# The small matmuls of a step gathered at its end, and the attention and expert work moved into the other halves of two PSUM banks

## The reference, cut to what matters

```python
# mixer, per sequence (chunks of 32 tokens in the reference; the kernel takes a sequence of 64 as one)
proj = input_states @ in_proj_w.T                 # gate, xBC, dt
xBC = silu(conv(moveaxis(xBC, 1, 2), 4 taps) + conv_b)
scores = einsum('bcihn,bcjhn->bcijh', Cc, Bc) * Ldec * dtc
y = einsum('bcijh,bcjhp->bcihp', scores, xc) + state part + D * x
g = y * silu(gate);  g = gg * rsqrt(mean(gg*gg) + eps) * norm_w    # 8 groups of 1024
x = x + g @ out_w.T
# attention: 8 kv heads, 4 repetitions, 16 dims, keys = values = ctx
scores = einsum('bsgrd,btgd->bgrst', xq, xk) / sqrt(16) + mask
x = x + einsum('bgrst,btgd->bsgrd', softmax(scores), xv)
# experts: 4 of rank 16, the best 2 of them weighted
x = x + sum_e gates[e] * (mid[e] @ B[e].T) * 4
```

## Time and profile before

| | |
|---|---|
| three runs | 3002.11, 3005.6, 3007.3 us |
| the profiled execution | 3009.73 us, span 3007.9 us |
| PE busy | 2905.6 us, 97% |
| DVE busy | 2024.6 us, 67% |
| ACT, POOL busy | 1366.0 us (45%), 1251.1 us (42%) |
| chain that ended last | PE 92%, DVE 5% |
| mean granted TensorE clock | 0.979 |

### The profile page before, as it was taken

One profiled execution on the slowest core, in us unless ns is written; L12 is line 12 of the kernel. 1 busy time (PEld: TensorE's weight loads), 2 busy tenths in 40 slices (PEclk: granted clock), 3 DMA queues, 4 the chain that ended last, 5 costly groups with the idle time before them and its releaser, 6 DMA issues.

```text
span 3007.9 us, 56310 instructions
## 1 busy us (share of the span) xinstructions
PE 2905.6 (97%) x22224; PEld 2292.7 (76%) x22224; DVE 2024.6 (67%) x3144; ACT 1366.0 (45%) x2025; POOL 1251.1 (42%) x820
## 2 busy tenths in 40 slices
PE   3999999999999999999999999999999999999986
PEld 2777777777778777787877778787777877777764
DVE  4787777787666657776666665777566665666656
ACT  2556556555443443443444444344344344444422
POOL 2666666666333433333333333433333343333332
PEclk7999999999999999999999999999999999999985
DMA  5787787778655655655665565655565565565510
GB/s 180 258 269 266 256 270 254 244 261 268 194 173 184 189 179 168 189 184 174 203 188 174 188 189 161 190 181 176 185 197 185 172 191 182 168 194 183 172 36 15
DMA packets 179267, 578.27 MB, mean 192 GB/s; under 512 B 25216, under 2 KB 31872, under 8 KB 170816
## 3 DMA queue, kind: packets, MB, share of 16 engines
q1 hardware_dynamic: 179008, 574.66, 59.8%
HBM read 460.29 MB, written 114.29 MB: 191 GB/s over the span
## 4 chain that ended last, share of the span: by engine, by line
PE 92%; DVE 5%; ACT 1%; issue 1%; DMA 1%; POOL 0%; SPq 0%; ACTq 0%; DVEq 0%; POOLq 0%
PE p_in L431 53%; PE p_out L431 23%; PE p_y L431 10%; PE p_in L510 4%; DVE cv L1125 1%; PE p_y L601 1%; DVE o_ring L1067 1%; ACT w_ring L763 0%; DVE acb L1184 0%; DVE sm L1271 0%; DVE cpar L1108 0%; ACT o_ring L763 0%; DVE sc L1259 0%; DMA decay<-cum_scr 0%; PE p_y L620 0%
## 5 line engine op out<-in xcount | busy, mean ns | idle before, releaser
L431 PE MATMUL p_in<-xnb,w_ring 128*128 128x512 f32 x6912 | 1735.3, 401 | 13.8 <-DVE cv L1125 9.6
L431 PEld LDWEIGHTS p_in<-xnb,w_ring 128*128 128x128 f32 x6912 | 1263.5, 189 | 286.3 <-issue 14.7
L1447 POOL TENSOR_TENSOR g_lo<-g_f,g_hi 128x512 fp32r<-128x512 f32 x256 | 375.6, 1467 | 1248.5 <-ACT g_hi L763 1248.5
L1125 DVE SCALAR_TENSOR_TENSOR cv<-p_in,cpar,cv 128x504 f32<-128x504 f32 (+2 forms) x960 | 703.4, 733 | 118.7 <-ACT cv L763 94.9
L431 PE MATMUL p_out<-o_ring,g_hi 128*128 128x512 f32 x2048 | 648.1, 397 | 0.0
L763 ACT ACTIVATE cv<-p_in,cpar 128x512 f32<-128x512 f32 x320 | 247.9, 777 | 734.3 <-PE p_in L431 689.7
L1160 DVE SCALAR_TENSOR_TENSOR t_y<-x_t,dpar,p_y 128x256 f32<-128x256 f32 x512 | 222.8, 476 | 397.6 <-PE p_y L431 395.2
L431 PEld LDWEIGHTS p_out<-o_ring,g_hi 128*128 128x128 f32 x2048 | 382.4, 188 | 91.1
L763 ACT ACTIVATE sg<-p_in 128x512 f32<-128x512 f32 x256 | 153.5, 600 | 628.3 <-PE p_in L431 628.2
L431 PE MATMUL p_out<-o_ring,g_lo 128*128 128x512 f32 x1024 | 405.4, 396 | 0.0
L1149 DVE TENSOR_TENSOR x_tok<-p_in,dts 128x512 f32<-128x512 f32 x256 | 176.9, 691 | 299.0 <-PE p_in L510 295.5
(11 more groups left out here) (233 smaller groups left out, 2244.3 us busy)
## 6 DMA issues: line engine op xcount, KB each, us to landing
w_ring<-ws_scr SPq DMA_DIRECT2D x432, 512.0 KB, 3.4
o_ring<-ows_scr SPq DMA_DIRECT2D x192, 512.0 KB, 3.4
ws_scr<-w_ring SPq DMA_DIRECT2D x144, 512.0 KB, 4.8
decay<-cum_scr SPq DMA_DIRECT2D x128, 512.0 KB, 6.6
raw_w<-wt SPq DMA_DIRECT2D x144, 256.0 KB, 4.1
ows_scr<-o_ring SPq DMA_DIRECT2D x64, 512.0 KB, 6.2
raw_o<-owt SPq DMA_DIRECT2D x64, 256.5 KB, 5.4
acb<-x SPq DMA_DIRECT2D x3, 1024.0 KB, 7.8
```

The costliest lines, as they stand in the source:

```text
L431: return nc.tensor.matmul(o, lhsT=l, rhs=r, start=first, stop=last)
L1125: ins = V.scalar_tensor_tensor(acc[:, :, t:SEQ], src[:, :, 0:SEQ - t], cpar[:, 5 * m + 3 - t:5 * m + 4 - t], acc[:, :, t:SEQ], ALU.mult, A ...
L1447: T(g_lo[:, c % 2, :], g_f[:, c % 2, :], g_hi[:, c % 2, :].bitcast(F32), ALU.subtract).then_inc(glo_done, 1)
```

## The change

The work is the same; places, buffers and order change.

- `p_in`, `p_y` and `p_out` become single tensors, and every slot now writes to `free`, columns 256 to 511 of the two `p_y` banks, beside the columns that `heads` uses. A slot of PE no longer waits for `yread`. Instead ACT's slot waits for it (`heads_read`) before it reads the banks, and DVE's `skipped` waits until the step's slot is written (`slot_written`).
- PE's step is A, B, `project`, `heads`, slot, `to_tokens`. At an iteration's beginning `heads(7)` of the iteration before comes after `project(6)`, and `state_products` after the first half of `project(7)`.
- DVE's step is `conv`, then the clamps, `decayed` and `early`, then `skipped`, `gated`, `x_tokens`. ACT reads its slot before `g_high` and `square`.
- `scores` take one repetition at a time (4 matmuls, four slots: steps 5, 6, 7 and the next iteration's -1) instead of two; `probs` too (steps 4 to 7); `values` move to slot -1 of the next iteration, and with them `attended`, `residual` and what follows. `delta` moves from step 2 to 1, `maxima` from step 7 of the even iteration to step 1 of the odd one, POOL's `shifted` from before step 1 into it, `result` from the end of step 2 into it (before `skipped`), `low` behind `decayed` in even iterations. `step_sizes` are 24 matmuls of 256 columns instead of 12 of 512. Softplus's parts are spread anew over g = 5 and 6.

```diff
 
 
-        p_in = [outer.enter_context(nc.psum_tensor(f"p_in{b}", [P, 512], F32)) for b in range(2)]
+        p_in = outer.enter_context(nc.psum_tensor("p_in", [P, 2, 512], F32))
         p_y = outer.enter_context(nc.psum_tensor("p_y", [P, 2, 512], F32))
-        p_out = [outer.enter_context(nc.psum_tensor(f"p_out{b}", [P, 512], F32)) for b in range(QT)]
+        p_out = outer.enter_context(nc.psum_tensor("p_out", [P, QT, 512], F32))
+        free = p_y[:, :, 256:512]
...
 
         LOOP_TILES = QT * (NTB - 1)
...
             for w in range(STAGES + QT - 1):
-                if LATE + w < STAGES:
...
+                for k in LATE[w] if w < len(LATE) else ():
+                    stage(k, LOOP_TILES - 1, loop_tile, (p_y[:, :, 0:256], p_y[:, :, 256:512]))
...
+                if k in (5, 6, 7) and t is not None:
+                    pe.wait_ge(sc_done, REP * t + k - 4)
...
+                if k == 1 and former(u) is not None:
                     pe.wait_ge(yo_done, u)
...
-                pe.wait_ge(yread, CPG * n + k)
...
-                if k == 6 and u is not None:
-                    values(u, S, y0)
...
+                    scores(t, S, k - 5, free)
+                if k == -1 and u is not None:
...
+                if k == 1 and former(u) is not None:
+                    delta(u - 1, S, free)
...
                     project(CPG - 2, *back)
+                    heads(CPG - 1, *before, n - 1)
+                    slot(-1, tb, g)
                 else:
                     pe.wait_ge(dtr_done, 1)
...
                 unit(3, tb, g, n)
+                if begun:
+                    project(CPG - 1, *back, range(0, 2))
+                    slot_read(-1, tb, g)
                 state_products(n)
                 if begun:
-                    project(CPG - 1, *back, range(0, 2))
                     mean_squares(n - 1)
+                slot(0, tb, g)
                 to_tokens(0, n)
 
                 unit(4, tb, g, n)
-                heads(0, tb, g, n)
                 unit(5, tb, g, n)
                 if begun:
                     project(CPG - 1, *back, range(2, QT))
-                slot(1, tb, g, n)
+                heads(0, tb, g, n)
+                slot(1, tb, g)
                 to_tokens(1, n)
 
                 for k in range(2, CPG):
                     unit(2 + 2 * k, tb, g, n)
-                    heads(k - 1, tb, g, n)
                     unit(3 + 2 * k, tb, g, n)
                     project(k - 2, tb, n)
-                    slot(k, tb, g, n)
+                    heads(k - 1, tb, g, n)
+                    slot(k, tb, g)
                     to_tokens(k, n)
...
-                    g_high(k - 1, n)
...
                     if k == 7 and not final(n):
...
+                    slot(k, tb, g, n)
+                    g_high(k - 1, n)
                     square(k - 1, n)
                     refill(k)
-                    slot(k, tb, g)
...
+                        act.wait_ge(yread, CPG * n + k)
...
+            def slot_written(k, tb, g):
...
+                if k == 1 and former(u) is not None:
+                    dve.wait_ge(dl_done, u)
...
+                if k == 0 and former(t) is not None:
...
+                    expert_row(t - 1, S)
...
+                if k == 1 and u is not None:
+                    maxima(u, S)
+                if k == 2 and former(u) is not None:
+                    result(u - 1, S, free)
...
+                if k == (3 if g % 2 == 0 else 2) and tile is not None:
                     normal(tile, xnt[:, :], xt[:, :], tile)
+                if k == (4 if g % 2 == 0 else 3) and tile is not None:
+                    tok = slice((tile % QT) * P, (tile % QT + 1) * P)
+                    low(tile, xnb[(tb + 1) % 2][:, 1, :, tok], xnb[(tb + 1) % 2][:, 0, :, tok], free)
...
+                if is_at(tb, g, 5) and k in (0, 2, 3, 6, 7):
+                    softplus(tb + 1, {0: (0, 1), 2: (2,), 3: (3, 4, 5), 6: (6, 7), 7: (8, 9, 10)}[k])
+                if is_at(tb, g, 6) and k in (0, 1, 3):
+                    softplus(tb + 1, {0: (11,), 1: (12,), 3: (13,)}[k])
...
+                if k == -1 and former(t) is not None:
+                    attended(t - 1, S, free)
+                    residual(t - 1, S, x1_of(t - 1))
+                if k in (5, 6, 7) and t is not None:
+                    scored(t, S, k - 5, free)
+                if k == -1 and u is not None:
+                    scored(u, S, 3, free)
...
-                    ins = V.scalar_tensor_tensor(S.sc[:, half, j, :, :], banks[j].rearrange("p (g t) -> p g t", g=KV), HD ** -0.5,
-                                                 am[:, :].unsqueeze(1).broadcast_to([P, KV, SEQ]), ALU.mult, ALU.add)
+                    ins = V.scalar_tensor_tensor(S.sc[:, r, 4 * j:4 * j + 4, :], area[:, j, :].rearrange("p (g t) -> p g t", g=4), HD ** -0.5,
+                                                 am[:, :].unsqueeze(1).broadcast_to([P, 4, SEQ]), ALU.mult, ALU.add)
...
                 dve.wait_ge(par_done, n + 1)
                 conv(0, n)
+                conv(1, n)
                 if begun:
...
+                    skipped(CPG - 1, n - 1)
                     gated(CPG - 1, n - 1)
                     dve.wait_ge(xtok_done, CPG * n)
...
                     dve.wait_ge(dtk_done, 2)
+                late(-1, tb, g)
+                skips(g, n)
                 steps(tb, g)
 
                 conv(2, n)
+                early(0, tb, g)
+                slot_written(0, tb, g)
                 products(n)
                 dve.wait_ge(cbt_done, n + 1)
                 decayed(0, n)
...
                 for k in range(1, CPG):
-                    skipped(k - 1, n)
                     conv(2 + k, n)
-                    gated(k - 1, n)
                     if k == 2:
                         clamped(1, n)
                     if k == 4:
@@ -1377,6 +1456,9 @@
                     if k == 6 and not final(n):
                         clamped(0, n + 1)
                     early(k, tb, g)
+                    slot_written(k, tb, g)
+                    skipped(k - 1, n)
+                    gated(k - 1, n)
                     x_tokens(k, n)
...
+                    dve.wait_ge(qk_done, REP * t + 2 * (k - 2) + 2)
+                    for a in range(2):
+                        scored(t, S, 2 * (k - 2) + a, areas[a])
...
-                if u is not None:
-                    shifted(u, S)
                 for k in range(1, CPG):
                     refill(k - 1)
-                    if k == 5 and t is not None:
+                    if k == 1 and u is not None:
+                        shifted(u, S)
...
```

511 lines of the change are left out of this document (271 added, 240 removed).

## The result

| | before | after |
|---|---|---|
| median of six runs | 3006.88 us (3002.11 to 3008.66) | 3073.16 us (3070.12 to 3074.9) |
| profiled execution, span | 3007.9 us | 3068.4 us |
| 800 to 2890 us without PE busy | 0.2 us | 31.2 us |

Ratio 1.022, 95% interval 1.0207 to 1.0234: slower by 66 us, outside the range forecast (2992 to 3058). The profiled execution of after, 3070.16 us, is one of the two lowest of its six, that of before, 3009.73, lies above all of its six; so the two traces differ by 60.4 us, and it is these that are taken apart.

A forecast was written before the change was run, and what follows sets the result against it. PE, never waiting in blocks 1 to 3, was taken as the bound, each late operation costing its full length. 12 + 1.6 + 10.6 + 10 + 4 + 3 - 7.7 - 3 = +30.5 on 3009.7: 3040 profiled, 3036 median; range 2992 to 3058.

The forecast's parts named there:

- Regrouping on PE: Each PE step: A and B join, but transposes follow small tiles; an empty step stays 9.58 us, so 0 in all.
- small slots: Slots in small tiles, now next to the heads, save 0.16 us each, four per tile over 12 tiles: 7.7 us gained.
- beginnings: At an iteration's beginning the state products no longer cut the projection in two: 0.10 x 32, 3 us gained.
- step sizes: 24 matmuls of 256 columns cost 0 to 2.8 us more, three times in the loop; together +3.
- Place 1: Odd iterations, step 1 to 2: heads wait 1.1 us for the result behind POOL's chain and DVE's clamp; 11 iterations, +12.
- `low`: Step 4 of g = 0 and 2, blocks 1 and 2: `low` behind `decayed` makes heads wait 0.4 x 4, +1.6.
- Softplus: g = 5 and 6 of blocks 1 and 2: softplus's parts make DVE late, 5.3 x 2, +10.6.
- Block 0: ACT's splitting behind `g_high` and `square` delays DVE: 17 us less what waits now, bounded by 0 and 25, taken as +10.
- Tail: Behind the loop: one more stage of DVE work, later `x_tokens`, scores read in twice the instructions; +4, between 0 and 8.
- leaving the heads is free, and DVE is in time: Rival, chance 0.2: end of each step saves 0.12 us over 216 steps, 26 us, with 10.7 of the slots.
- the four places: Odd iterations' step 1 to 2, `low` behind `decayed`, softplus, block 0: where DVE is late; under 37 us together, the rival decides.
- an empty step of 9.6: Sign in the profile after: a PE step with an empty slot takes 9.6 us; 9.5 or less would refute the forecast.

The follow-up runs named there:

- the waits mended: Changed kernel, new order kept, with splits behind `tap0`, result first, half maxima, `low` ahead of `decayed`, softplus part 5 moved, `x_tokens` ahead of `decayed` in step 0: 3014.87 us.
- the experiment: Changed kernel, but in step 2 of odd iterations DVE adds the experts' result before the clamp that waits for POOL: 3060.59 us.
- block 0 left as it was: Kernel of 3014.87 us with block 0 in the order before, then `decayed` and softplus's first parts there put right and softplus spread anew in blocks 1 and 2: 2996.98 us.
- the half maxima: Changed kernel with the result ahead of the clamp, and the maxima of the first two repetitions taken in step 7 of the even iteration: 3047.57 us.
- the moved splits: Changed kernel, but in block 0 ACT's splits come one step later, behind `tap0`, and DVE's `o_low` behind the convolution: 3050.09 us.
- the run with the maxima late: Changed kernel, but in step 1 of odd iterations DVE's maxima come behind the accumulation and POOL's shift behind the differences: 3114.52 us.

## Why the prediction was wrong

**The direction and the kind of loss were right, the size was not**: +30.5 forecast, +60.4 between the traces. By its own terms:

- *Regrouping on PE, 0, and small slots, -7.7, beginnings, -3, step sizes +3.* Right in direction, too timid. The empty step fell by 0.06 us; heads followed by scores take 0.52 instead of 0.63. In n = 8 to 31 PE's work fell by 14 us, and by 18 with the waits mended, where these terms made about 8. (The 5.66 us for B with its projection were read where the next iteration's unit follows, not transposes; where transposes follow they are 5.67, so nothing hangs on it.)
- *Place 1, odd iterations, +12.* The chain was right to 0.2 us: 1.27 us in each of 10 iterations of this stretch and once behind it. Its reverse in the experiment gave 12.6. Missed was `x_tok` in the same ten iterations, 0.40 in step 0 (scores are read ahead of it) and 0.54 in step 1 (the gate stands still beside POOL's shift), 0.95 x 10, and 2.26 in step 1 of n = 9: 11.8 in all. The step "follow `skipped` 0.79, `gated` 0.60" took a duration from a place where POOL was idle.
- *`low`, +1.6*: 2.5.
- *Softplus, +10.6*: 3.7, of which 1.39 twice in g = 6 (2.2 forecast) and 0.48 twice in g = 5 (3.1 forecast).
- *Block 0, +10 between 0 and 25: this is the step that failed.* It measured 40.7. The prediction found the right row ("ACT's splitting now stands behind `g_high` and `square`") and charged it mainly against `x_tokens`. But the late `tap0` and `o_low` come ahead of the convolution, and so of `x_t`: "the transposes of step 0 by 0.3, eight times" became 16.6 us of waits for `x_t` in 16 places. The experiments divide the 40.7 in two ways: 28.4 hang on the order and 12.3 on the new steps of the slots; and of it all about 8.4 come with POOL's `w_low`, which stretches clamp and `o_low`. And 8 us are not waits but work that takes longer, about 7 of them at half clock behind waits, which the prediction did not count at all.
- *Tail, +4*: 1.1.

The sum for n = 8 to 31, about +16 by these terms and +17.0 measured, came out right by luck, because errors cancel: softplus 7 too much and PE's gain 6 too small on one side, the 11.8 of `x_tok` left out on the other. Of the rivals, "leaving the heads is free, and DVE is in time" fell in both halves: DVE was late, and PE's gain is 14 us, not 26 and 10.7. Its mechanism has a core though: with the waits mended and block 0 left as it was, the change ends 11.8 us below the kernel before, and with block 0 changed too 7.5 above it. "It decides once the four places lose under 37 us together" was thus too generous: what they have to stay under is PE's gain, 14 to 18 us. The range failed since its upper bound took block 0's end at 25, which was a count of the same places, not a bound from outside.

The rule of the Trainium skill, TensorEngine Tiling (Array Packing), Key Properties, that a change of tiling mode drains TensorE, held: regrouping the heads alone saved next to nothing (0.06 us a step), and slots of 64x64 tiles next to the heads saved more (0.37 with the heads between A and B set against heads at the end).

B did not wait in ordinary steps of blocks 1 to 3, and POOL's differences stand right behind shift and `g_low`, as written; an empty step of 9.6 did not come.

Open: of the 11.9 us that the half maxima gave in n = 8 to 31, 2.6 are neither waits nor half clock; which part of block 0's 12.3 us belongs to which slot, and how the 18.4 us of the moved splits divide between ACT and DVE, was not separated.

## What to carry to other kernels

When an operation moves to the end of a step, follow what is queued behind it on each engine round to the next step's first operation, and charge the delay to every consumer on the way, not to the last one alone. Work that was free in a gap must be costed beside its new neighbour: here a VectorE instruction on two SBUF operands took up to five times its length beside GpSimd (3.44 us for 0.69). And a bound for the part of a program with the least slack should come from its total of spare time, not from the places one has thought of.

## What the hardware showed beyond the forecast

- Beside POOL's instruction the gate went from 0.69 to 2.20 us and once to 3.44, and the clamp, in the run with the maxima late, from 1.22 to 2.85, each ending 0.55 to 1.1 us behind it; instructions with a PSUM operand kept their length. Where DVE started 0.04 us first, it was POOL's that stretched, from 1.29 to 1.81.
- Behind a wait of 5 us TensorE took 5.30 us for 2.95 us of matmuls, granted clock 0.60. In n = 8 to 31 of the changed kernel the clock fell behind the one wait of 2.26 us (twelve matmuls in 4.4 us), and not behind the 38 waits of 0.4 to 1.4 us.
- The sixteen matmuls of heads in 64x64 tiles take 0.52 us to the next start where the scores follow in such tiles, and 0.63 before every other group.
